# Waits between the third batch's slot writes, and value columns made ahead of the last batch's prefix sums, in a four-layer gated kernel

## What is computed

```
x = x + tanh(g_xattn[0]) * attention(layernorm(x), ctx)          # 16 heads, 512 x 512 a batch
# the experts of layer 0, over all 2048 tokens of layernorm(x):
probs = softmax(x @ gate_w.T);  topk_p, topk_i = top_k(probs, 8);  topk_p /= sum(topk_p)
onehot = one_hot(topk_i.reshape(-1), 64);  pos = cumsum(onehot, axis=0) - 1   # place within its expert
dispatch[expert, pos] = token's row (dropped where pos >= 64)
y = (silu(dispatch @ w_gate.T) * (dispatch @ w_up.T)) @ w_down.T
out[token] = sum over its 8 of y[expert, pos] * topk_p        # times tanh(g_ffn[0]), added to x
```

## Time and profile before

| | before |
|---|---|
| runs | 2944.91 us median (2941.24 to 2959.34) |
| the profiled execution | 2945.35 us; its span from first to last instruction 2943.6 us |
| PE busy | 2481.0 us (84%) |
| DVE busy | 1828.4 us (62%) |
| ACT busy | 1170.7 us (40%) |
| POOL busy | 755.3 us (26%) |
| granted TensorE clock, mean | 0.920 |

### The profile page before, as it was taken

One profiled execution on the slowest core, in us unless ns is written; L12 is line 12 of the kernel. 1 busy time (PEld: TensorE's weight loads), 2 busy tenths in 40 slices (PEclk: granted clock), 3 DMA queues, 4 the chain that ended last, 5 costly groups with the idle time before them and its releaser, 6 DMA issues. The chain is left out here.

```text
span 2943.6 us, 35609 instructions
## 1 busy us (share of the span) xinstructions
PE 2481.0 (84%) x12608; PEld 1335.9 (45%) x12608; DVE 1828.4 (62%) x4072; ACT 1170.7 (40%) x2095; POOL 755.3 (26%) x462
## 2 busy tenths in 40 slices
PE   6888972865888699889899979989988989997996
PEld 2333331323555344545554635554454545463554
DVE  5667745246867474477767357748437875835774
ACT  1433430212323153265544146635325653514662
POOL 1002352520000042043323023414203432402441
PEclk8999985875878799999999999999999999999998
DMA  7411006974200200244320124430023442012442
GB/s 226 136 37 21 11 15 206 316 249 150 87 8 3 106 1 1 87 108 119 97 79 8 73 61 118 116 111 11 8 88 100 116 108 79 1 52 71 110 125 73
DMA packets 112959, 257.06 MB, mean 87 GB/s; under 512 B 36198, under 2 KB 56294, under 8 KB 106762
## 3 DMA queue, kind: packets, MB, share of 16 engines
q1 hardware_dynamic: 93978, 220.26, 24.8%
q10 hardware_dynamic: 12656, 25.97, 3.6%
q0 software_dynamic: 6144, 8.48, 1.0%
HBM read 119.81 MB, written 29.69 MB: 51 GB/s over the span
## 5 line engine op out<-in xcount | busy, mean ns | idle before, releaser
L858 POOL TENSOR_SCALAR pbuf<-pbuf,recip 128x1024 f32<-128x1024 f32 x128 | 364.5, 2848 | 946.0 <-DVE recip L762 946.0
L807 ACT ACTIVATE pbuf<-ps,least 128x1024 f32<-128x1024 f32 x256 | 284.3, 1113 | 295.3 <-DVE least L755 219.5
L755 DVE CUSTOM_DVE_ANT_0 ps<-ps,mask 128x1024 f32<-128x1024 f32 x256 | 307.9, 1244 | 140.2 <-PE ps L687 139.2
L584 POOL TENSOR_SCALAR pbuf<-pbuf,recip 128x512 f32<-128x512 f32 x128 | 200.2, 1576 | 459.7 <-DVE recip L505 459.7
L687 PE MATMUL ps<-kH,qT 64*128 64x512 f32 x1024 | 267.4, 642 | 49.8 <-ACT pbuf L807 47.0
L712 PE MATMUL ps<-work,vh 128*64 128x256 f32 x2048 | 251.9, 390 | 0.0
L555 ACT ACTIVATE pbuf<-ps,least 128x512 f32<-128x512 f32 x256 | 172.7, 686 | 155.6 <-DVE least L495 155.6
L769 DVE STREAM_TRANSPOSE pbuf<-pbuf 128x2048 f32<-128x2048 f32 (+1 forms) x128 | 226.3, 1768 | 0.0
L1554 ACT ACTIVATE early<-ps 128x1536 f32<-128x1536 f32 x86 | 123.9, 1441 | 200.9 <-PE ps L1369 191.7
L1632 DVE TENSOR_REDUCE mh<-ps 128x3 f32<-128x1536 f32 x86 | 150.0, 1744 | 63.8 <-PE ps L1358 61.2
L712 PEld LDWEIGHTS ps<-work,vh 128*64 128x64 f32 x2048 | 138.3, 138 | 95.2 <-issue 36.6
(11 more groups left out here) (371 smaller groups left out, 4054.7 us busy)
## 6 DMA issues: line engine op xcount, KB each, us to landing
work<-pbuf SPq DMA_DIRECT2D x784, 96.0 KB, 2.5
work<-pbuf ACTq DMA_DIRECT2D x240, 96.0 KB, 2.9
early<-in_L_wgu SPq DMA_DIRECT2D x22, 768.0 KB
expert_rows<-zero_rows SPq DMA_DIRECT2D x16, 1024.0 KB, 11.5
yg<-expert_rows SPq DMA_DIRECT2D x16, 1024.0 KB, 6.0
early<-in_L_wd SPq DMA_DIRECT2D x22, 384.0 KB
arena<-in_L_wo SPq DMA_DIRECT2D x8, 1024.0 KB, 8.8
arena<-in_L_wff SPq DMA_DIRECT2D x4, 2048.0 KB, 9.3
```

The costliest lines, as they stand in the source:

```text
L584: nc.gpsimd.tensor_scalar(x, x, recip[:, n % 8:n % 8 + 1], None, mult).then_inc(probs_ready[1], 1)
L755: nc.vector.tensor_tensor_reduce(out=x, in0=x, in1=mask, scale=1.0, scalar=FMAX, op0=add, op1=ALU.min, accum_out=least[:, n % 8:n % 8 + 1])\
L807: nc.scalar.activation(to, x, ACT.Exp, bias=least[:, n % 8:n % 8 + 1], scale=-1.0, accum_out=sums[:, n % 8:n % 8 + 1]).then_inc(taken, 1)
L858: nc.gpsimd.tensor_scalar(unit(n), unit(n), recip[:, n % 8:n % 8 + 1], None, mult).then_inc(pool_divided, 1)
```

## The change

Two edits, both in layer 0.

First, `scatter` has a new argument `alone`, which `hand_out` sets for the third batch (b = END - 1). With it, each write first waits on the semaphore of the write before it, for the count that this one's landing gives.

Second, what `last_table` did on DVE ahead of the marks moves into a function of its own, `last_columns`, called right behind the instructions that make `before`, that is ahead of the wait for PE's prefix sums. It takes along the wait for the exponents (`exps`). `mark(0)` now follows `key`, in one loop with the other seven.

```diff
-        def scatter(b, tiles, step=lambda n: None):
+        def scatter(b, tiles, step=lambda n: None, alone=False):
 
             for t in tiles:
                 for k in range(TOPK):
                     step(t * TOPK + k)
+                    before = (b * NT + t) * TOPK + k - 1
+                    if alone:
+                        nc.gpsimd.wait_ge(scattered[before // 4 % 2], 64 * (before // 8) + 16 * (before % 4 + 1))
                     group = ((b * NT + t) * TOPK + k) // 4
                     if k % 4 == 0 and group >= 2:
                         nc.gpsimd.wait_ge(scattered[group % 2], 64 * (group // 2))
...
-                        scatter(b, [t], lambda n: pool.wait_ge(scores_kept, min(base[b] + 50 + n // 2 + 1, NSTEP)))
+                        scatter(b, [t], lambda n: pool.wait_ge(scores_kept, min(base[b] + 50 + n // 2 + 1, NSTEP)), b == END - 1)
...
-                def last_table(place, t0):
+                def last_columns():
                     for t in range(NT):
                         nc.vector.tensor_tensor_scan(rep[:, t, :], sel[:, t, :], zero_rows[:, 0:E], -1.0, add, add)
                     v.wait_ge(exps, B)
...
-                    v.wait_ge(job_kept, place + 1)
-                    mark(0).then_inc(onehot_ready, 1)
                     link(last)
                     nc.vector.tensor_copy(column(0), by_expert(rep))
...
                     nc.vector.tensor_tensor(column(3), by_expert(lg), column(2), subtract).then_inc(vals_ready, 1)
-                    for i in range(1, HALVES):
+
+                def last_table(place, t0):
+                    v.wait_ge(job_kept, place + 1)
+                    for i in range(HALVES):
...
                     last.then_inc(before_ready, 1)
+                    if b == END:
+                        last_columns()
                     k = ("place", b, 0)
```

## The result

| | before | after |
|---|---|---|
| median | 2946.3 us of 6 runs (2941.24 to 2959.97) | 3005.62 us of 6 runs (3000.54 to 3013.69) |
| the profiled execution | 2945.35 us, span 2943.6 | 3003.29 us, span 3001.3 |
| granted clock, mean | 0.920 | 0.912 |

The ratio is 1.0191, with a 95% interval from 1.0168 to 1.0213: slower by 56 us (49.5 to 62.8) by the ratio, and by 59.3 us between the medians. The forecast was 2989.5 us, 44.2 us above before, in a range that ended at 3004. The median lies 1.6 us past that end; the ratio applied to the forecast's own starting point, 2944.91, gives 3001 us, within it. The direction, the place and the round of a write were right, and the loss, 59.3 against 44.2, was 15 us larger than forecast.

What follows compares the result with a forecast made beforehand. Bound: a relay from layer 0's routing to the experts: GpSimd's slot writes, SP's table load and weights, the block's end. Serial writes add 50.7 us, less 6.5 of slack: 2945.35 + 44.2, rounded to 2989.5 us; range 2978 to 3004.

Steps and rivals of the forecast that it cites:

- The round: Third batch's slot writes on GpSimd: landing 2.14 plus restart 0.78 gives 2.92 us instead of 1.284; 31 add 50.7 us.
- the two ends of its bounds: Limits for one slot write's round: 2.38 us, adding 34.0 us over 31 rounds, and 3.15 us, adding 57.8 us.
- the rival of long rounds: Each restart of a slot write is dearer than measured: 51.3 us net loss, 2996.7 us; chance 0.07.
- The slack: At the end of layer 0's attention and routing block, SP finishes 6.5 us before DVE; deducted from the 50.7 us.
- SP's chain: SP's table load, early weights, `x_d` and `rows_d`, to the landing of `normed_rows`: keeps its 39.05 us, ending at 547.1.
- the columns: DVE's scans and casts moved ahead of `key`: at best 3.8 us gained on DVE, worth nothing before the table wait.
- short rounds: GpSimd's start overlaps the landing, so each slot write costs 2.14 us: 20.0 us net loss, 2965.4 us; chance 0.10.
- not slower: Waits cost next to nothing and DVE regains 17.0 us: 2938.9 us, decided by rounds below 1.49 us; chance 0.05.

## Why the prediction was right, and where its size was off

**The round: right.** 2.14 us for the landing and 0.78 for the restart gave 2.92; the trace shows 2.89 to 2.94 where DVE makes no marks, but for the first round, 3.15, and one of 3.22. The nearest rows of before carried the term, and the two ends of its bounds (2.38 and 3.15) can both be dropped. What is shown is the sum of the two halves; no row shows where in a round the landing lies, and the 2.14 hold SP's own restart. That a write's cost overlaps between queued writes and adds up between serial ones, which the forecast took over, the runs show: 1.28 us a write queued, 2.92 in series. The mean of all 31 rounds, 97.93 / 31 = 3.16, looks like the rival of long rounds, but it isn't: that rival made every restart dearer, and of the excess of 7.4 us over 31 x 2.92 the five rounds beside the marks carry 6.9 (487.29 - 465.78 - 5 x 2.92).

**The slack: wrong.** "SP's chain therefore has 6.5 us of slack to DVE's chain, and not more" was read from one execution and taken for the kernel. Two further traces of before have SP last, with 0.2 us. The step that failed is the deduction of 6.5 us from 50.7. A hint stood in the earlier trace rows: a gap put down to "remote", with no instruction of this core behind it, need not be a property of the code. The forecast also said that DVE would be prompt if GpSimd left pauses. It was, but in before's other executions it was as prompt beside writes without a pause, so the pauses are not the reason. What made DVE late in that one execution stays open.

**The marks: left out.** The forecast put DVE's marks ahead of about 481 us and the writes up to 506, so that it had both side by side, and asked no price for it. In the forecast's trace of before they did not meet (the marks began at 477.94, the last write at 455.20), again because DVE was late there. The price: 97.93 - 31 x 2.92 = 7.4 us by the forecast's round, 97.93 - 91.39 = 6.5 us against the trace with the marks moved away. It rests on the traces, since the 8.4 us between those medians are not clear of their spread.

The forecast hadn't asked the rule that bears on it. The Trainium skill (SBUF — State Buffer, the section "SBUF: two separate sides") says that VectorE and GpSimd share a pair of ports as an exclusive lock, taken for a whole instruction, also by a VectorE instruction with two inputs in SBUF against a GpSimd operation that reads SBUF. The trace agrees as far as it goes: the mark (L1230) reads `key` and `slot_no`, the write reads `info` and `place`, all four in SBUF; a mark takes 2.2 us, and a write beside it is up to 3.08 - 0.97 = 2.1 us longer, by about one mark. The runs show that the marks lengthen the writes; that a lock of ports is the means, no run here shows.

**The sum.** 50.7 + 7.4 = 58.1 us for the writes, no slack deducted: 58.1 against the 59.3 between the medians and the 56 of the ratio, inside its interval (49.5 to 62.8 us). The forecast's 44.2, below that interval, was short by these two terms, 6.5 and 7.4. The interval is 13 us wide, and it holds 50.7 (no slack, no marks) and 51.6 (both) as well: the times rule out the forecast's sum, but the two terms rest on the traces. For the missing slack one time speaks too: with two writes in flight the writes are 9.75 us longer, and 9.75 - 6.5 = 3.3 us lies below the interval of that kernel's ratio (7.7 to 17.7 us).

The two profiled executions differ by other parts. The next block's first issue moves from 503.64 to 564.75, by 61.1 us: the writes begin 9.0 us later (415.41, 424.39), take 58.1 longer, and the way from the table's load to that issue is 6.0 shorter (46.30, 40.29). The kernel before alone varies in the first and the last of these: its second trace begins its writes at 424.39 too, and has a way of 42.9. Behind that issue both executions take nearly the same, 2440.0 and 2436.6 us of the span, so the loss lies where the forecast put it.

**SP's chain, the columns, the rest: right.** The chain kept its length to 0.3 us (39.34), but so close a match is luck: the kernel before has 42.0 and 43.2 in its other traces, and over all traces of these kernels with SP's old order the way from the table's load to the next block is 40.3 to 46.3 us long. The columns close the gap of 3.83 us ahead of `key`, save 3.5 to 3.9 us on DVE and nothing at the end. Of the rivals, short rounds and "not slower" fall with the rounds of 2.9; the kernel that waits for the write two before has, away from the marks, a mean of 1.485 us a write, just the 1.49 at which the forecast's "not slower" was to begin. It was slower by 10.2 us: its marks met the writes too, which take 49.54 us in its trace, 9.75 more than in the earlier trace rows, and no slack was there to swallow them.

## What to carry to other kernels

A wait for each landing turns a queue of transfers into a relay, and its price is one start, landing and restart for each, less the pace before; both halves can be read from single rows of a trace that has no such wait, at the load that those rows had (2.92 us a round at rest here, 7 to 8 beside bulk loads). A slack of a few microseconds between two chains should be seen in more than one execution before it enters a sum, above all if the later chain is late for a cause that isn't in the code. And when a change stretches one engine's work over another's, ask what the two do to each other there, not only which ends last; here, too, the better change was to give the idle DMA engines their loads during the writes.

## What the runs showed that was not expected

- An indirect write beside DVE's marks takes GpSimd 1.3 to 3.1 us instead of 0.97 in the change, and up to 3.45 in the traces of the other kernels. DVE's marks are no longer for it (17.70 us for eight beside the writes, 17.71 alone).
- One small write's round from start to restart, 2.92 us when the DMA engines rest, is 7.2 to 8.2 us beside the early weights. The same writes without a wait for each landing lose little (45.07 and 45.64 us for 32, where the earlier trace rows have 39.79), partly beside the marks and partly at the older wait ahead of every fourth write.
- DVE's 15.39 us of idle time in the earlier trace rows are in one of three traces of before, and in that one alone. The start of the third batch's writes, too, lies between 411.7 and 427.7 us in the traces of all these kernels, before any of their edits acts; the three traces of before alone spread from 415.4 to 424.4.
